# Weighted values of the joined attentions: one block of four key blocks per group among the next group's column jobs, in place of two blocks of two

## What is computed

```python
q, k, v = split_heads(x @ Wq), split_heads(x @ Wk), split_heads(x @ Wv)    # 16 heads x 8
dot = jnp.einsum('bqhd,bkhd->bhqk', q, k) * scale
dot = jnp.where(causal, dot, -inf)
attn = softmax(dot, axis=-1)
out = jnp.einsum('bhqk,bkhd->bqhd', attn, v)                               # "weighted values"
return x + out.reshape(b, t, 128) @ Wo
```

## Time and profile before

| | us |
|---|---|
| median of three runs | 3970.35 |
| all runs | 3969.64, 3970.35, 4764.65 |
| profiled execution, its time | 3971.17 |
| its span (first to last instruction) | 3969.2 |
| TensorE busy | 3730.0 |
| weight loads of TensorE (overlap it) | 2470.3 |
| VectorE busy | 2296.7 |
| ScalarE busy | 1752.8 |
| GpSimd busy | 825.0 |

### The profile page before, as it was taken

How to read it: one execution, slowest core, us unless ns; L and a number is a source line. 1 busy time by engine, 2 the same in 40 slices (tenths; PEclk the granted TensorE clock), 3 DMA queues, 4 the chain that set the end, 5 groups by cost and what they waited for, 6 DMA issues and landing times.

```text
span 3969.2 us, 77473 instructions
## 1 busy us (share of the span) xinstructions
PE 3730.0 (94%) x30495; PEld 2470.3 (62%) x30495; DVE 2296.7 (58%) x7498; ACT 1752.8 (44%) x3562; POOL 825.0 (21%) x1374
## 2 busy tenths in 40 slices
PE   6999999988999999998899999999889999999988
PEld 4555567665555667766555556776655555677665
DVE  5546454677545545477664554547676455445776
ACT  3425233466432523346643252335664334233556
POOL 3103023321210302332021020233302102033330
PEclk9999999999999999999999999999999999999999
DMA  2000000000000000000000000000000000000000
GB/s 85 1 1 1 1 1 1 2 2 1 13 1 1 1 1 1 1 2 2 1 13 1 1 1 1 1 1 2 2 7 7 1 1 1 1 1 1 2 2 9
DMA packets 20222, 17.32 MB, mean 4 GB/s; under 512 B 2620, under 2 KB 19469, under 8 KB 19853
## 3 DMA queue, kind: packets, MB, share of 16 engines
q1 hardware_dynamic: 19853, 12.25, 1.1%
HBM read 10.15 MB, written 2.10 MB: 3 GB/s over the span
## 4 chain that ended last, share of the span: by engine, by line
PE 73%; DVE 10%; POOL 7%; ACT 7%; issue 3%; DVEq 0%; POOLq 0%; ACTq 0%; SPq 0%
PE banks L1155 9%; PE banks L1169 8%; PE banks L1165 8%; PE banks L1004 5%; PE banks L1043 5%; POOL work L539 4%; PE banks L1058 4%; PE banks L983 3%; PE banks L877 3%; PE banks L1209 3%; PE banks L1407 3%; PE banks L1269 2%; ACT work L827 2%; ACT work L821 2%; PE banks L1420 2%
## 5 line engine op out<-in xcount | busy, mean ns | idle before, releaser
L1584 DVE CUSTOM_DVE_ANT_0 work<-banks,mask_row 128x512 f32<-128x512 f32 (+3 forms) x1024 | 434.1, 487 | 272.9 <-PE banks L1004 272.7
L732 ACT ACTIVATE work<-banks 128x512 f32<-128x512 f32 (+1 forms) x384 | 227.5, 597 | 642.9 <-PE banks L1165 634.1
L495 POOL TENSOR_TENSOR rstd<-rstd,half 128x4 f32<-128x4 f32 x65 | 65.5, 1008 | 2083.8 <-DVE rstd L1516 2083.8
L707 ACT ACTIVATE work<-banks 128x384 f32<-128x384 f32 (+1 forms) x768 | 359.9, 536 | 255.4 <-PE banks L1043 254.9
L1043 PE MATMUL banks<-work 32*128 32x384 f32 (+3 forms) x2048 | 446.4, 467 | 6.5 <-DVE work L1584 3.9
L1676 DVE TENSOR_TENSOR work<-work,banks 128x512 f32<-128x512 f32 (+1 forms) x384 | 260.7, 686 | 272.6 <-PE banks L1169 272.6
L1004 PE MATMUL banks<-work 32*128 32x384 f32 (+3 forms) x2048 | 408.3, 458 | 10.6 <-ACT work L693 6.4
L1155 PEld LDWEIGHTS banks<-wd,work 128*128 128x128 f32 (+1 forms) x3072 | 359.3, 191 | 49.1 <-issue 49.1
L1155 PE MATMUL banks<-wd,work 128*128 128x128 f32 (+1 forms) x3072 | 361.1, 274 | 0.0
L506 POOL TENSOR_SCALAR_AFFINE_SELECT work<-work 128x128 f32<-128x128 f32 (+1 forms) x768 | 253.3, 333 | 461.3 <-ACT work L707 437.7
L1043 PEld LDWEIGHTS banks<-work 32*128 32x128 f32 x2048 | 244.0, 184 | 76.9 <-ACT work L707 42.6
(11 more groups left out here) (316 smaller groups left out, 6667.8 us busy)
## 6 DMA issues: line engine op xcount, KB each, us to landing
wg<-in_L_ffn_Wg_dram SPq DMA_DIRECT2D x1, 1376.0 KB
wu<-in_L_ffn_Wu_dram SPq DMA_DIRECT2D x1, 1376.0 KB
x_a<-in_L_attn_a_x_dram SPq DMA_DIRECT2D x5, 256.0 KB, 2.8
x_b<-in_L_attn_a_x_dram SPq DMA_DIRECT2D x4, 256.0 KB, 3.8
wd<-in_L_ffn_Wd_dram SPq DMA_DIRECT2D x2, 512.0 KB
out_dram<-x_a SPq DMA_DIRECT2D x4, 256.0 KB, 2.3
out_dram<-x_b SPq DMA_DIRECT2D x4, 256.0 KB, 2.3
wk_l<-in_L_attn_a_Wk_dram SPq DMA_DIRECT2D x1, 512.0 KB, 7.2
```

The source lines that it names most:

```text
L707: eng.activation(prob4[:, g % 2, hh, C_AT[j]:C_AT[j] + C_N[j]], bank(column_bank(c))[:, 0:C_N[j]], ACT.Exp).then_inc(s_exp, 1)
L1584: m = eng.tensor_tensor_reduce(out=summed[:, k % 2, col:col + N], in0=bank(bk)[:, col:col + N], in1=mask_row[:, T - N:T], scale=1.0, scala ...
```

## The change

The first of the two blocks, key blocks 0 and 1 at `at == 10`, is kept for the last group only. The block at `at == 3` of the next group now takes all four key blocks. For groups 0 to 6, 8 matmuls (16 records) are moved five row jobs and five column jobs later; what `weigh_group` waits for at `at == 3` is what the second block waited for already. The last group (7) keeps its two blocks.

```diff
@@ pe_attn @@
                 if k >= LEAD and g >= 1 and at == 3:
-                    weigh_group(g - 1, [2, 3])
+                    weigh_group(g - 1, [0, 1, 2, 3])
                 if k % ROWS4 == 2 and k >= ROWS4:
...
-                if k >= LEAD and at == 10:
+                if k >= LEAD and at == 10 and g == GROUPS - 1:
                     weigh_group(g, [0, 1])
             weigh_group(GROUPS - 1, [2, 3])
```

## The result

| | us |
|---|---|
| before, median of 6 runs | 3970.45 |
| after, median of 6 runs | 3989.39 (3986.76 to 3991.59) |
| ratio, 95% interval | 1.0048 (1.0034 to 1.0062) |
| profiled execution after: time, span | 3986.76, 3984.8 |

The change makes the kernel 19 us slower, 0.48%. One of the six runs of before, 4764.65 us, is a slow one, far above the other five, and is left out of the ratio.

What follows compares the result with a forecast made beforehand. The prediction took TensorE, busy 94% of the span, to bound the kernel. Usual groups 0, group 0 3.0, group 6 10.1 and clock 3.0 gave +16.1 us on the median of 3970.35: 3986 us, range 3973 to 3999.

Steps and rivals of the forecast that it cites:

- Moving the block costs nothing in a usual group: Groups 1 to 5, 40 blocks: maxima's break 1.53 us shorter, middle break 1.53 us longer, sum 0.
- No switch is saved: The break at k mod 12 = 2 keeps its transposes and projection, so no tiling-mode switch, 0.11 us each, is gained.
- The rival "faster": The joined block saves one or two switches, 6 to 12 us over 56 blocks: 3958 to 3964, chance 0.06.
- Group 0: At k = 26 the first column job waits for VectorE's `shift_q`: 0.38 us in each of 8 stages, 3.0 us.
- Group 6: At k = 98 the joined block waits behind GpSimd's `pow` and diagonal: 5 x 1.53 + 3 x 0.81 = 10.1 us.
- The price of 0.81 us for three stages: Smaller loss at the stage end in the 3 of 8 stages where the clock had fallen there before.
- The clock: Longer idle time at stage ends brings none to eight more clock falls, about 1.5 us each; two taken, +3 us.
- The sum: All terms over the whole kernel: 0 + 3.0 + 10.1 + 3.0 = +16.1 us.
- The rival "no change": The chain of the `pow` moves with TensorE, groups 0 and 6 lose nothing: 3970, 3966 to 3974, chance 0.12.
- "Much slower": The clock falls 1.5 us at each of 56 joined blocks, 84 us: 4067 with the waits, chance 0.02.

Runs made afterwards that it cites:

- e3_join_6: Against the kernel before, only group 6 joined, 8 of the 56 blocks: 3987.86 us, ratio 1.005.
- e4_after_pow_later: The changed kernel, all seven groups joined, with GpSimd's `pow` behind the diagonal of column job 83 instead of 82: 3964.72 us, ratio 0.9994.
- e10_join_6_pow: Against the kernel before, only group 6 joined and GpSimd's `pow` behind the diagonal of column job 83: 3963.9 us, ratio 0.9994.
- the fills: The changed kernel with matmuls whose results nothing reads, ahead of group 6's joined block: 3994.49 us with 8, 3988.47 us with 4.

## Why the prediction was right

It said 3986 us, 3973 to 3999; measured 3989.39. The place and the mechanism of the loss were right; two of its smaller steps were not, and part of the nearness is luck. Step by step:

- **Moving the block costs nothing in a usual group.** Right. 1.53 us off one break and 1.53 on the other was the sum; the trace has the block at 2.29 against 0.78, 1.51. The groups between k = 38 and k = 86 keep their lengths to 0.02 us, and k = 86 to 98 gains 0.14 us: -1.2 us in all. This I had wrong. "No switch is saved" rested on the block's neighbour being a projection of the same 128 x 32 form; at k = 86 the neighbour is L1084, a 128 x 128 form, so with the block a change of form leaves that break, which gets 1.64 us shorter in place of 1.53. The rival "faster" has these 8 of 56 blocks right, 1.2 us. The first part of the prediction's reasoning, that a phase's length runs from its own start, is what the 3.30 us before and after show.
- **Group 0.** Right: 3.0 us expected, 2.6 measured (0.33 a stage for 0.38). The wait is for `shift_q`, as said.
- **Group 6.** Right in place, mechanism and size: 1.51 us for 1.53 at full clock, the wait 1.87 us for 1.7. The column jobs came sooner by the whole 1.64 us of the block, not by 1.53, and 0.23 + 1.64 is 1.87. The experiments `e3_join_6`, `e4_after_pow_later` and `e10_join_6_pow` are the proof: this join alone has the loss, and moving the `pow` out of the queue ahead of the diagonal takes it away. The price of 0.81 us for three stages did not apply, because in no stage of the changed kernel did the clock fall at the transposes: all eight paid 1.51, 12.1 us for the 10.1. Where it did fall there, in stage 2 of `e3_join_6`, the block starts 5.38 us after the transposes, for the 388.30 - 382.85 = 5.45 of the prediction, and the end is 0.7 us longer than in the same stage of before.
- **The clock.** The number came out near, 3.8 us for 3, but as the sum of other parts. The prediction kept the three falls that before had and added two. In the trace the three falls at the transposes (1.5 us each) are gone and five new ones at the joined block (1.6 to 1.7 us each) stand in their place. Two was a choice between none and eight, so the hit is luck: `e3_join_6` shows falls in all eight stages, six at the joined block behind the same wait and two at the transposes. The mechanism behind it is not settled: the fills took the falls away and gave nothing back. The 16.2 us by which the stage ends grew are 12.1 from the block behind the wait, 3.8 from these falls and 0.4 from one more slow output. In stage 8, for example, the end is 1.96 us longer, 1.51 from the block; the rest is that from the output's transposes (L924) to the projection (L933) it takes 1.80 us in place of 1.34, at the fallen clock.
- **The sum.** 16.1 us were forecast, against 15.6 between the profiled spans and 19 between the medians. The stage ends were 3.1 us more than their 13.1, and the 1.2 us at k = 86 and 2 us outside the stages took as much back; that is luck too.
- The rival "no change" fails on the chain, which did not move with TensorE. "Much slower" needed a fall at each join: in the trace the clock falls nowhere between k = 26 and the transposes of k = 98.

## What to carry to other kernels

A block of work that looks movable may be the cover for a chain on other engines; before it is moved behind a wait, read when what it waits for is really ready, and what is queued ahead of that on its engine. Here nearly the whole price of the move came from 8 of 56 blocks, through a `pow` of GpSimd in front of an instruction that did not need it, and putting the two the other way round took it back. A change that is neutral in the loop's body should be checked at its first and last turn, where the other engines do something else.

## What the runs showed of the hardware

A wait of 1.87 us ahead of the joined block was followed by the lower clock in five of eight stages (block 3.70 or 3.98 us in place of 2.29). With 8 or 4 matmuls put into it, waits of 0.03 or 0.90 us were left and the clock stayed at 1.00 there in all stages where it had not fallen before. But the kernel did not get shorter: at the idle times of the output, some 10 us later, the clock fell and stayed at 0.50 for at least 8 us (1140 to 1148, with 8 fills), where the changed kernel had 1.00 again in 1146 to 1150. The Trainium skill's page "TensorE: Matmul & The Clock Gate", section "HAM oscillation — how this bites in real kernels", tells of waits that let the clock drop. The falls at the joined block, there with the wait and gone without it (the later `pow`, wait 0.20 us), agree with it. That the later falls get longer with the fills is seen in the one trace of each of the two kernels that have them, and unexplained.

The wait is not all that decides. In the kernel before, TensorE is busy 3.52 of the 4.00 us ahead of the transposes of k = 98 in stage 1 and in stage 2 alike, and the clock falls at them in stage 2 and not in stage 1. Windows of TensorE, stage 1 and stage 2:

```profile
131.45:135.45 4.00, 3.52 (x36) 1.00 0.01 2
378.85:382.85 4.00, 3.52 (x37) 0.98 0.01 2
```
